# Attention with scores formed twice and values in column tiles, in a six-layer kernel on one core

## The reference, cut to what matters

```
h   = layernorm(x)
q, k, v = split(h @ w_qkv.T)                # 16 heads of 8 features
scores  = q @ k.T / sqrt(8)                 # -inf unless j <= i and i - j < 64
attn    = softmax(scores)                   # over keys
x       = x + (attn @ v) @ w_out.T + b_out
```

## Time and profile before

| | us |
|---|---|
| median of 3 runs (lowest, highest) | 846.19 (845.01, 850.92) |
| profiled execution, its time | 846.63 |
| its span | 844.9 |
| mean granted clock of TensorE | 0.753 |
| busy in the span: PE / DVE / ACT / POOL | 638.6 / 461.3 / 279.1 / 319.7 |

### The profile page before, as it was taken

One profiled execution on the slowest core, in us unless ns is written; L12 is line 12 of the kernel. 1 busy time (PEld: TensorE's weight loads), 2 busy tenths in 40 slices (PEclk: granted clock), 3 DMA queues, 4 the chain that ended last, 5 costly groups with the idle time before them and its releaser, 6 DMA issues.

```text
span 844.9 us, 12071 instructions
## 1 busy us (share of the span) xinstructions
PE 638.6 (76%) x4330; PEld 417.1 (49%) x4330; DVE 461.3 (55%) x912; ACT 279.1 (33%) x501; POOL 319.7 (38%) x252
## 2 busy tenths in 40 slices
PE   3958788878887887796895653677776886786897
PEld 2747676757675766574673221222332332234675
DVE  3663443344334442444325727999788887963521
ACT  1313434333533352142121548233334233320211
POOL 2420000000000050104441124599799797981522
PEclk9985656565656565697987875699878988998886
DMA  5000000000000000000000006444245244000000
GB/s 137 0 1 2 0 0 0 0 0 0 0 0 0 0 1 2 0 1 0 0 1 0 0 6 230 175 199 198 101 174 223 99 200 180 19 1 0 14 12 25
DMA packets 12021, 42.27 MB, mean 50 GB/s; under 512 B 2830, under 2 KB 8476, under 8 KB 9948
## 3 DMA queue, kind: packets, MB, share of 16 engines
q1 hardware_dynamic: 11180, 41.43, 12.9%
q10 hardware_dynamic: 816, 0.53, 0.2%
HBM read 40.65 MB, written 1.31 MB: 50 GB/s over the span
## 4 chain that ended last, share of the span: by engine, by line
PE 37%; DVE 24%; issue 20%; POOL 11%; ACT 6%; DMA 1%; DVEq 1%; POOLq 0%; SPq 0%; ACTq 0%
DVE hst L833 6%; PE bk L583 6%; DVE smax L487 5%; PE bk L399 4%; PE bk L556 4%; POOL hC L892 4%; PE bk L550 3%; PE bk L408 3%; PE bk L570 3%; PE bk L946 3%; POOL rows L361 2%; DVE rows L492 2%; DVE rows L720 2%; POOL powers L290 2%; ACT bk L1014 2%
## 5 line engine op out<-in xcount | busy, mean ns | idle before, releaser
L892 POOL TENSOR_TENSOR hC<-hst,rows 128x1024 f32<-128x1024 f32 x64 | 148.9, 2354 | 35.6 <-DVE hst L833 35.6
L283 POOL TENSOR_TENSOR veps<-mv,lneps 128x4 f32<-128x4 f32 (+1 forms) x36 | 7.0, 194 | 385.2 <-DVE mv L255 385.2
L946 PE MATMUL bk<-hC,ident 128*128 128x512 f32 x256 | 136.7, 672 | 15.3 <-POOL hC L892 15.1
L833 DVE TENSOR_TENSOR_SCAN hst<-bk,dBu 128x1024 f32<-128x1024 f32 x64 | 144.2, 2274 | 4.6 <-POOL dBu L881 4.6
L1014 ACT ACTIVATE bk<-delta,aneg 128x1024 f32<-128x1024 f32 x64 | 71.5, 1117 | 149.7 <-DVE hst L833 149.7
L946 PEld LDWEIGHTS bk<-hC,ident 128*128 128x128 f32 x256 | 53.4, 216 | 80.2 <-issue 49.0
L439 ACT ACTIVATE rows<-bk 128x512 f32<-128x512 f32 x64 | 38.2, 597 | 111.7 <-PE bk L399 111.7
L661 ACT ACTIVATE rows<-rows 128x512 f32<-128x512 f32 x64 | 40.3, 630 | 102.6 <-DVE rows L492 102.6
L487 DVE TENSOR_REDUCE smax<-bk 128x4 f32<-128x512 f32 x64 | 43.7, 683 | 49.5 <-PE bk L556 49.5
L819 DVE TENSOR_TENSOR dBu<-bk,du 128x1024 f32<-128x1024 f32 x48 | 57.7, 1202 | 20.5 <-PE bk L930 20.3
L583 PE MATMUL bk<-rows 128*64 128x9 f32 x1024 | 54.3, 236 | 11.1 <-ACT rows L669 11.1
(11 more groups left out here) (155 smaller groups left out, 1055.1 us busy)
## 6 DMA issues: line engine op xcount, KB each, us to landing
rows<-c_rows SPq DMA_DIRECT2D x16, 2048.0 KB, 7.1
rows<-c_rows SPq DMA_DIRECT2D x4, 1024.0 KB, 9.5
x<-in_x_dram SPq DMA_DIRECT2D x4, 256.0 KB, 4.8
out_dram<-x SPq DMA_DIRECT2D x4, 256.0 KB, 2.3
w1s<-in_w_dram ACTq DMA_DIRECT2D x1, 256.0 KB, 3.9
w2s<-in_w_dram ACTq DMA_DIRECT2D x1, 256.0 KB, 6.5
wup<-in_upT_dram SPq DMA_DIRECT2D x1, 256.0 KB
wdn<-in_downT_dram SPq DMA_DIRECT2D x1, 256.0 KB
```

Of the source, the lines that this page charges most:

```text
L833: nc.vector.tensor_tensor_scan(hst[k % 3][:, :], dA[k % 2][:, :], dBu[k % 3][:, :], 0.0, ALU.mult, ALU.add).then_inc(m2["scan"], 1)
L892: nc.gpsimd.tensor_tensor(hC[k % 4][:, :], hst[k % 3][:, :], crep[:, k % 12, :], ALU.mult).then_inc(m2["hC"], 1)
L946: last = nc.tensor.matmul(bk01[:, r * CH:(r + 1) * CH], ident[:, :], hC[k % 4][:, r * CH:(r + 1) * CH], start=False, stop=(k % NS == NS - ...
```

## The change

The attention is written anew, its tiles unrolled in all queues.

- LayerNorm, the transposition of x and the q and k products go by chunks of 512 tokens; v by half chunks. q, k and v of a sequence stay in memory (`qm`, `kT`, `va`), and the next chunk's are made during tiles 1 to 3 of a chunk, all through one PSUM bank, `psQ`.
- Scores are formed twice. First with queries on partitions, half of the heads at a time in banks 0 and 1, `bk01` (`scores`), only for the row maxima (`maxima`, 1024 elements). The 16 maxima per query, at 4 of 32 places each, are transposed (`transpose_max`), spread with the sign changed (`spread_max`), and then added to scores with keys on partitions (`masks`, `shifted`) in four banks, `ST`. Their exponential (`probs`, two activations of 1024) is already what `values` needs, so the transposes of probabilities, their copies and the subtraction are gone.
- `values` runs with 128 rows and 32 columns of the array, eight matmuls of 256 columns for v and eight for row sums by a matrix of ones, into `OD`, the same banks 0 and 1. `context` takes the reciprocal of 512 elements per partition, and multiplies; `project` needs no transpose, but four products with masked copies of w_out (`wom`) and the bias.
- The masks of the next tile stand before the transposition of its maxima in TensorE's order.
- VectorE now waits for `set_attn` too. In GpSimd's queue the clearing of `xb` and what follows it wait for the last attention update.

The diff, without the removed lines of the attention (they are in the code above):

```diff
-        qm = home(10960, HPG, P)
-        kT = home(11472, P // 2 + P)
-        va = home(11664, 2, H, HD + 1)
-        mask = home(12240, NT * P // 2).bitcast(BF16).rearrange("p (t k) -> p t k", t=NT)
...
+        qm = home(8192, HPG, T)
+        mexp = home(4608, HPG, P)
+        cx = home(5120, HPG, P)
+        rden = home(5632, HPG, P)
+        wom = home(6144, HPG, P)
+        mask1 = home(6656, P).bitcast(BF16).rearrange("p (f k) -> p f k", f=2)
+        maskT = home(6784, P).bitcast(BF16).rearrange("p (f s q) -> p f s q", f=2, s=2)
+        smaxp = home(6912, JG, 32)
...
+        va = u[:, :, :].rearrange("p h (w n) -> p (h w) n", n=P)
+        pT = g[:, 0, :].rearrange("p (j s n) -> p j s n", j=JG, s=2)
+        spare = delta[:, :, :].rearrange("p i l -> p (i l)")
+        kT = spare[:, 0:B * (64 + L)].rearrange("p (b n) -> p b n", b=B)
+        xw = spare[:, 2304:2304 + 2 * (64 + CH)].rearrange("p (c n) -> p c n", c=2)
...
+        def window(t, s):
+            return 2 * t + s
+        def by_half(t):
+            return t.rearrange("p a (s q) -> p s a q", s=2)
+        ST = bk2345[:, :].rearrange("p (j s a q) -> p j s a q", j=JG, s=2, a=HPG)
+        OD = bk01[:, :].rearrange("p (o s n) -> p o s n", o=2, s=2)
+        psM, psP = bk67[:, 0:P], bk67[:, P:2 * P]
...
+            def maxima(t, p):
+                dve.wait_ge(at["s"], 2 * t + p + 1)
+                if t > 0:
+                    dve.wait_ge(at["mt"], t)
+                nc.vector.tensor_reduce(smaxp[:, 2 * p:2 * p + 2, 0:HPG],
+                                        bk01[:, :].rearrange("p (j a k) -> p j a k", j=2, a=HPG), AX.X, ALU.max
+                                        ).then_inc(at["max"], 1)
+            def spread_max(t):
+                dve.wait_ge(at["mt"], t + 1)
+                if t > 0:
+                    dve.wait_ge(at["st"], t)
+                nc.vector.tensor_tensor(mexp[:, :, :], psM.rearrange("p (o q) -> p o q", o=1).to_broadcast([P, HPG, P]),
+                                        negd[:, :].rearrange("p (a o) -> p a o", o=1).to_broadcast([P, HPG, P]),
+                                        ALU.mult).then_inc(at["mexp"], 1)
             def context(t):
                 dve.wait_ge(at["pv"], t + 1)
+                nc.vector.reciprocal(by_half(rden), OD[:, 1, :, :].rearrange("p s (a q) -> p s a q", a=HPG)
+                                     ).then_inc(at["rden"], 1)
                 dve.wait_ge(at["rden"], t + 1)
+                if t > 0:
+                    dve.wait_ge(at["op"], t)
+                nc.vector.tensor_tensor(by_half(cx), OD[:, 0, :, :].rearrange("p s (a q) -> p s a q", a=HPG),
+                                        by_half(rden), ALU.mult).then_inc(at["cx"], 1)
             def update(t):
                 dve.wait_ge(at["op"], t + 1)
                 nc.vector.tensor_tensor(xs(t * D, D), psP, xs(t * D, D), ALU.add).then_inc(at["xupd"], 1)
+            for t in range(NT):
+                c, i = t // TPC, t % TPC
+                if t + 1 < NT:
+                    maxima(t + 1, 0)
+                if t > 0:
                     update(t - 1)
+                if i == 0 and c + 1 < NC:
+                    ln_first(c + 1)
+                if t + 1 < NT:
+                    maxima(t + 1, 1)
+                    spread_max(t + 1)
+                context(t)
+                if i == 0 and c + 1 < NC:
+                    ln_second(c + 1)
             update(NT - 1)
         def attn_pool(pool):
+            with pool.Fori(0, NC) as c:
+                ln_pool(pool, at, c, TPC, False)
...
+            def project_q(c):
+                pe.wait_ge(at["free"], 5 * c + 1)
+                nc.tensor.matmul(psQ, wqkv[:, 0:P], xw[:, c % 2, 64:64 + CH], start=True, stop=True
+                                 ).then_inc(at["full"], 1)
+            def project_k(c):
+                pe.wait_ge(at["free"], 5 * c + 2)
+                nc.tensor.matmul(psQ, wqkv[:, P:2 * P], xw[:, c % 2, 64:64 + CH], start=True, stop=True
+                                 ).then_inc(at["full"], 1)
+            def project_v(c, p):
+                pe.wait_ge(at["free"], 5 * c + 3 + p)
+                for n in range(4):
+                    at_ = (4 * p + n) * 64
+                    last = nc.tensor.matmul(psQ[:, n * P:(n + 1) * P], xw[:, c % 2, at_:at_ + P], wqkv[:, 2 * P:3 * P],
+                                            start=True, stop=True)
+                last.then_inc(at["full"], 1)
+            def scores(t, p):
+                c, b, r = t // TPC, t // TPB, t % TPB
+                pe.wait_ge(at["free"], 5 * c + 3)
+                if p > 0:
+                    pe.wait_ge(at["max"], 2 * t + 1)
+                elif t > 1:
+                    pe.wait_ge(at["cx"], t - 1)
+                for j in range(2):
+                    nc.tensor.matmul(bk01[:, j * CH:(j + 1) * CH], identb[:, :],
+                                     mask1[:, int(r == 0):int(r == 0) + 1, :].to_broadcast([P, HPG, P]),
+                                     start=True, stop=False, skip_group_check=True)
+                for a in range(HPG):
+                    for s in range(2):
+                        for j in range(2):
+                            g_ = 32 * (2 * p + j)
+                            last = nc.tensor.matmul(bk01[64 * s:64 * s + 64, j * CH + a * P:j * CH + (a + 1) * P],
+                                                    qm[g_:g_ + 32, a, t * P + 64 * s:t * P + 64 * s + 64],
+                                                    kT[g_:g_ + 32, b, r * P + 64 * s:r * P + 64 * s + P],
+                                                    start=False, stop=True, skip_group_check=True)
+                last.then_inc(at["s"], 1)
+            def transpose_max(t):
+                pe.wait_ge(at["max"], 2 * t + 2)
+                if t > 1:
                     pe.wait_ge(at["xupd"], t - 1)
+                nc.tensor.transpose(psM, smaxp[:, :, :].rearrange("p j a -> p (j a)"), ident[:, :]).then_inc(at["mt"], 1)
             def masks(t):
+                r = t % TPB
+                if t > 0:
+                    pe.wait_ge(at["p"], 2 * t)
                 for j in range(JG):
+                    nc.tensor.matmul(ST[:, j, :, :, :], identb[:, :],
+                                     maskT[:, int(r == 0), :, :].rearrange("p s (o q) -> p s o q", o=1
+                                                                           ).to_broadcast([P, 2, HPG, 64]),
+                                     start=True, stop=False, skip_group_check=True)
+            def shifted(t):
+                b, r = t // TPB, t % TPB
+                pe.wait_ge(at["mexp"], t + 1)
+                for j in range(JG):
+                    nc.tensor.matmul(ST[:, j, :, :, :], ones[32 * j:32 * j + 32, :],
+                                     by_half(mexp[32 * j:32 * j + 32, :, :]), start=False, stop=False,
+                                     skip_group_check=True)
                 for s in range(2):
                     for j in range(JG):
+                        last = nc.tensor.matmul(ST[:, j, s, :, :],
+                                                kT[32 * j:32 * j + 32, b, r * P + 64 * s:r * P + 64 * s + P],
+                                                qm[32 * j:32 * j + 32, :, t * P + 64 * s:t * P + 64 * s + 64],
                                                 start=False, stop=True, skip_group_check=True)
+                last.then_inc(at["st"], 1)
+            def values(t):
+                pe.wait_ge(at["p"], 2 * t + 2)
+                pe.wait_ge(at["free"], 5 * (t // TPC) + 4 + t % TPC // 2)
+                if t + 1 < NT:
+                    pe.wait_ge(at["max"], 2 * t + 4)
+                else:
+                    pe.wait_ge(at["cx"], t)
+                for s in range(2):
+                    for j in range(JG):
+                        nc.tensor.matmul(OD[32 * j:32 * j + 32, 0, s, :], va[:, window(t, s), 32 * j:32 * j + 32],
+                                         pT[:, j, s, :], start=True, stop=True)
+                for s in range(2):
+                    for j in range(JG):
+                        last = nc.tensor.matmul(OD[32 * j:32 * j + 32, 1, s, :], ones[:, 0:32], pT[:, j, s, :],
+                                                start=True, stop=True)
+                last.then_inc(at["pv"], 1)
+            def project(t):
+                pe.wait_ge(at["cx"], t + 1)
+                pe.wait_ge(at["mexp"], min(t + 2, NT))
                 for a in range(HPG):
+                    nc.tensor.matmul(psP, cx[:, a, :], wom[:, a, :], start=(a == 0), stop=False)
+                nc.tensor.matmul(psP, ones[0:1, :], bo[0:1, :], start=False, stop=True).then_inc(at["op"], 1)
+            for t in range(NT):
+                c, i = t // TPC, t % TPC
+                ahead = c + 1 < NC
+                shifted(t)
+                if i == 1 and ahead:
+                    transpose_x(c + 1)
+                if t + 1 < NT:
```

(94 more changed lines are left out.)

204 lines of the change are left out of this document (45 added, 159 removed).

## The result

The changed kernel takes 888.65 us (887.29 to 892.70, 4 runs) against 846.47 us: the ratio is 1.0497, interval 1.0445 to 1.0549. It is 5% slower; 831 us was forecast, with a range of 804 to 862. Some executions of a kernel have a lower granted clock than its others and take longer (e5: one of ten, 925.6 us at 0.60; e7: one of four; e10: two of four); medians are of all executions, ratios leave these out.

What follows compares the result with a forecast made beforehand. The prediction took attention to be bound by TensorE, with VectorE in turn. From 846.6 us it took 25.5 off for attention (258 us) and added 10.1 for GpSimd's delayed set-up: 831 us, range 804 to 862.

Steps and rivals of the forecast that it cites:

- The bound: Attention stage, 283.5 us: TensorE sets it, busy 229.7 us, with VectorE in turn; granted clock 0.58.
- The pieces: Priced parts of a new attention tile, such as score pass 1.7 us, values 2.2, maxima 1.3, reciprocal 3.6.
- the sum: Attention at full clock: 12.7 us per plain tile, 240 us for the stage with start, chunk work and end.
- a sixth of the difference: Clock charge in attention: between 240 us at full clock and 348 at half, 18 us added, giving 258.
- The scan: Stretch taken as nearest for the clock: TensorE waits each round, busy 192 of 250 us, granted 0.87.
- Rival 3: Attention: the pause under the reciprocal drops the clock in every tile; half the difference paid gives 867 us; chance 0.15.
- rival 4: Values in attention: column tiles go one after another, 5.2 us more in 16 tiles, 914 us; chance 0.04.
- GpSimd's set-up: Behind attention: set-up for later layers waits for the last update and delays the second MoE's LayerNorm, +10.1 us.
- Rival 1: Attention: the clock stays high, the pause after the shifted scores being under 3 us; 813 us; chance 0.15.
- Rival 2: Context in attention: reciprocal dearer by a quarter, 4.4 us, 13 us more in 16 tiles, 844 us; chance 0.15.
- Rivals 4, 5, 6: The sixth: GpSimd's set-up hides elsewhere, the 10 us don't come, 821 us, chance 0.03; the others have their own lines.
- rival 5: Context in attention: reciprocal at one element a step, 0.69 us, no pause left for the clock; 767 us; chance 0.05.

Runs made afterwards that it cites:

- e5: Kernel before the change, with two idle 256-column fp32 matmuls added per tile behind the last scores: 845.2 us, ratio 0.9956.
- e7: Changed kernel with row sums formed by head blocks (reciprocal of 128 elements) and GpSimd's set-up before the end of attention: 772.7 us, ratio 0.9067.
- e10: Changed kernel with two idle 256-column matmuls added per tile behind the shifted scores: 839.0 us, ratio 0.9816.
- e3: Changed kernel with four idle 256-column fp32 matmuls added per tile behind the shifted scores: 817.4 us, ratio 0.9627.
- e1: Changed kernel with GpSimd's set-up before the end of attention and xb cleared behind the second MoE: 874.8 us, ratio 1.0344.
- e2: Changed kernel with the 512-element reciprocal replaced by a multiplication by 1.0, leaving out the division: 777.3 us, ratio 0.9135.

## Why the prediction was wrong, point by point

- **The bound** was read rightly: TensorE and VectorE in turn; the new tile is a chain through banks 0 and 1.
- **The pieces** hold. Reciprocal 3.36 us (3.6 forecast from two short rows), maxima 1.22 (1.2), multiply 0.69 (0.69), masks and scores at the full clock 1.6 up to the next group (194.75 to 196.31 in e3; 1.7). Column tiles overlap as I took from L556: sixteen value and sum matmuls, 32 records, from 188.52 to 190.39 in e3, 1.9 us (1.7 and a change of tiling forecast). With the clock up, e3's plain tile is 12.5 us where the sum has 12.7. That its stage is 240.9 where the sum has 240 is partly luck: up to the first reciprocal it took 37.4 us (about 33 in the sum, but it ran at half until 80.8), and the next 14 tiles with the chunks' work 188.5 (192.8 in the sum).
- **The step that failed** is the clock: "As the falls begin in its own pauses, I charge a sixth of the difference: 240 + 18". Measured, the stage is 312.3, and (312.3 - 240)/108 is 0.67 of the difference. That a fall would begin in the wait was right. That so little would be paid behind it was wrong: the fall lasts 10 us in the tile shown (233.60 to 243.84) and up to 17 in others, over most of both score passes, the projection and the masks, so most of TensorE's part of the chain is run at the lower level. The scan, which I took as the nearest row, is not near. There fp32 matmuls of 512 columns on the whole array (L946) follow each wait, and the twelve falls that begin in its 250 us last 3.4 or 6.8 us each, behind waits of up to 6.9 us. The old attention was nearer: it stood at 0.50 for 23.9 us over two waits of 1.91 us. One fall of each in the trace of before, by timeline and by window:

```profile
188.74 0.45 PE L529 MATMUL bk<-ident,xnT 128*128 128x128 f32 x1 [1.91 <-DVE x L497]
...
556.17 0.60 PE L930 MATMUL bk<-s,sel 96*128 96x512 bf16 x2 [2.19 <-DVE dBu L819]
```

```profile
188.50:212.39 23.89, 20.01 (x191) 16.54 (x191) 10.75 (x22) 10.21 (x25) 0.74 (x2) 0.50 0.00 0
557.14:560.55 3.41, 3.41 (x6) 1.25 (x5) 3.41 (x3) 1.12 (x1) 3.41 (x2) 0.50 0.00 0
560.55:563.97 3.42, 3.42 (x9) 1.43 (x8) 3.42 (x3) 1.12 (x1) 2.88 (x2) 1.00 0.61 230
```

That the kind of work behind the wait makes this difference is argued from these rows; no run separates it. Rival 3 is what happened, with two thirds paid where it named a half; its chance of 0.15 was too low. With rival 4's 0.04 it is also more than the 0.18 that the sum of chances gave to slower.
- **GpSimd's set-up**: +10.1 forecast; the gap grew by 9.7, and e1 took it back. The first ternary layer's +3.1 no term of the forecast had.
- **Rival 1** (high clock, 813) is what e3 gives with work added: 817. Its ground, a pause under 3 us, was met and did not help: the pause was 2.37 us in plain tiles, and all 15 distances between two reciprocals have part of their time at 0.50. **Rival 2** (dearer reciprocal) is out: 3.36 us is 6.25 ns an element beyond the 16 of L477, and not dearer than the two short rows said. The Trainium skill (VectorE: DVE Perf Modes, First, the fixed hardware budget) has a divide with a repeat count of eight; at its 0.96 GHz I estimate 8.3 ns an element from that. The trace does not agree, and the measurement decides. **Rivals 4, 5, 6** did not occur; e2, which puts rival 5's 0.69 us in, took 777 where it has 767.
- **Own range**: 862 would have needed rival 3 at less than half. With the clock's two sums 108 us apart, one sixth on one row's authority was no basis for a range of 58 us.

## What to carry to other kernels

Where a chain leaves TensorE without work for two microseconds in each round, price what stands behind the wait at the lower clock, not the wait itself, unless a row shows that very work bringing the clock back. First shorten what it waits for (here an elementwise reciprocal over values of which three quarters are never used), then ask whether real work can stand in the wait. And look at what a new memory overlap makes wait: a set-up that was hidden became 10 us of bare path.

## What the runs showed of the hardware that I had not expected

Idle matmuls in a wait made the kernel 8% faster (ratio 1.0497 to 0.9627), and a clock that rose from 0.58 to 0.71 in the old kernel gave 0.4% (e5). The reciprocal's time grows evenly: 0.18, 0.26, 0.96 and 3.36 us for 4, 16, 128 and 512 elements per partition.
